# Rotary products of the queries on four column groups of TensorE, and weight preparation that waits for its own loads

## The chip, the core and the metric

The kernel runs on one core of a Trainium2 chip. A core has five engines that run side by side, each with its own stream of instructions: PE (TensorE, matrix products), ACT (ScalarE, activation functions and copies), DVE (VectorE, elementwise work, scans, reductions), POOL (GpSimd, slower elementwise work) and SP (SyncE, which here only issues DMAs). They are tied together by semaphores alone. Products land in PSUM, which has eight banks of 128 partitions by 512 float32; everything else lies in SBUF, on 128 partitions. The metric is the device time of one execution in microseconds (us), lower is better.

## What is computed

Eight sequences of 512 tokens with 256 channels go through four blocks, each `x = x + layernorm(block(layernorm(x)))`:

```python
# 1 attention with a compressed key/value and one rotary part shared by all 16 heads
c_kv   = x @ W_kv_down                                   # 256 -> 128
k_rope = rotary(c_kv @ W_k_rope); q_rope = rotary(x @ W_q_rope)      # 32 wide
rotary(x) = concat([x1*cos - x2*sin, x2*cos + x1*sin])   # x1, x2 the halves of 32 channels
scores = (q . k per head + q_rope . k_rope) / sqrt(48);  causal softmax;  @ v;  @ W_o
# 2 feed-forward 256 -> 1024 -> 256, ternary weights rebuilt in the kernel
#   scale = mean|w| by row, tern = clip(round(w/scale)); h = x @ (tern*scale).T + gate * x @ v.T @ fast_b.T @ u.T
#   out = ternary(w_proj) @ relu(h)**2
# 3 mixer: z = conv(x @ W_in), decays by a running sum, cos and sin of k*theta, weighted prefix scans, silu, @ W_out
# 4 feed-forward relu(x @ W1 + b1) @ W2 + b2
```

## The kernel before

Three chains of work are woven into each engine's stream. Chain `a` is the attention of one sequence ("batch" b), chain `d` holds the dense parts of the other three blocks, chain `m` is the mixer. A fourth chain `p` prepares the weights once, at the start. While chain `a` works on batch b, chains `d` and `m` work on batches b-1 and b-2. `chains()` lists the items of each chain in order, and the table `MERGE` says for each engine how many items to take from which chain in turn ("a8 p a2" is eight items of `a`, one of `p`, two of `a`). An engine executes its stream strictly in this order: an item that must wait holds everything behind it on its engine. `merged()` expands the table and `run()` calls `do` for each item (or `prepare` for those of `p`), and `between()` once before the first item of `d` or `m`.

The attention of a batch begins with a prologue on PE: `xT` (transposes of the input), `ckv`, `q` (two halves), `qr` (the rotary query product), `k`, `kr` (the rotary key product), `v`, `base`. Its 32 rotary channels are needed twice, once plain and once with the halves swapped, so the weights `wqr` and `wkr` hold both versions, 64 columns. `rotate` on DVE then multiplies 32 partitions of the result with the cosines and the next 32 with the sines (both in the table `rope`), and adds the two (L1340, L1341, L1344). `base` (L910) multiplies the rotated queries by the rotated keys for each of the four blocks of 128 queries, up to the diagonal. A product takes one of three PSUM banks in turn and waits until the bank was emptied.

Then 40 units of scores follow: `S` (PE L922), a fused add and maximum on DVE (L1410), the exponential on ACT (L1176), `T` (transposes, PE L930, copied by ACT L1183), `PV` (PE L948), which writes four groups of 32 columns of the array in turn. Queries and keys for `S` are split in three bf16 pieces by ACT (L1162, L1165), DVE (L1356) and POOL (L755, L757), sent to DRAM (L685) and read back into the tile `stack` (L636, six DMAs for a group of four heads).

The mixer of a batch takes on ACT the waves `fold`, `cos`, `sin` (L1239, L1243, L1246), on DVE `turn`/`frac` (L1468, L1478), `scan` (L1487) and `mix` (L1496) in 16 units of two scans and one mix, and on PE four `gather` (L1016). The ring of wave tiles is small: the `turn` of channels 4 to 7 needs gathers 0 and 1 first. In batches 0 and 7 `turn` is done by ACT (L1234). ACT holds one table set at a time; changing between exponential and sine is an instruction of its own, ACT_TABLE_LOAD.

At the start SP issues 33 loads in one row. Those for the attention count on the semaphore `loaded_first`. All others, from the ternary weights `raw_fc` to the bias `b2r`, count on one semaphore `loaded`, and the preparation on PE (L1049), ACT (L1272), POOL (L802) and DVE (L1533) waits until all of them have landed. Preparation works as `ternary` (ACT sums |w|, L1274; POOL compares and scales, L809 to L818), `prep` 0 to 15 (PE products and transposes, copied out by ACT or DVE) and `tables`.

## Time and profile before

| | us |
|---|---|
| median of 3 runs | 1410.93 |
| lowest and highest run | 1410.14, 1413.29 |
| the profiled execution | 1407.21 |
| its span, from first to last instruction | 1405.4 |

The profile is of one execution, so sums of durations are held against 1407.21; 1.8 us of it lie outside the span. It is 3.7 us below the median of the runs. The profile lists busy time by engine and by source line, a timeline, what each engine waited for, and the chain of work that ended last. PE is busy 87% of the span, DVE 78%, ACT 75%, POOL 24%, and the mean granted TensorE clock is 0.949 of the full one. Chains `d` and `m` have no work in the first 100 us; chain `a` has none after about 1180 us, when the mixers of batches 6 and 7 and their dense parts still run.

### The profile page before, as it was taken

To read this page: it belongs to the slowest core of one execution; us is meant where nothing else is said; L and a number is where in the kernel's file an instruction comes from. 1 tells how busy PE (TensorE), PEld (TensorE's weight loads), DVE (VectorE), ACT (ScalarE), POOL (GpSimd) and SP (SyncE) were. 2 spreads that over 40 slices of the span, in tenths; PEclk is the share of its full clock that TensorE was granted. 3 is DMA by queue.
4 is the path that set the end of the run, shared out by engine and by line. 5 is a ranking of instruction groups with operands and counts; after the bars stand their busy time and mean duration, and the time that the engine had idled before them with its cause. 6 is when DMAs were issued, how large, how long until landed. Compare 5 with 4: busy or idle time off the path is not lost.

```text
span 1405.4 us, 22661 instructions
## 1 busy us (share of the span) xinstructions
PE 1227.4 (87%) x7820; PEld 774.3 (55%) x7820; DVE 1101.7 (78%) x2259; ACT 1054.7 (75%) x2107; POOL 336.7 (24%) x317
## 2 busy tenths in 40 slices
PE   5889987888899998999999997998999998874767
PEld 2565664364546565666646764565646755542444
DVE  3683358779988988988888997898788998998940
ACT  4784789689789878798778888597778889547532
POOL 3943203400121303220134001430032201511021
PEclk9799999999999999999999999999999999996879
DMA  8404114412252105520334131511352131103000
GB/s 260 99 13 101 28 24 137 108 50 61 70 135 61 31 1 150 130 53 1 124 80 107 24 100 45 136 31 24 108 124 57 31 92 47 45 19 126 23 16 15
DMA packets 72019, 101.49 MB, mean 72 GB/s; under 512 B 10641, under 2 KB 44065, under 8 KB 71905
## 3 DMA queue, kind: packets, MB, share of 16 engines
q1 hardware_dynamic: 71904, 100.03, 27.2%
q8 instruction: 64, 1.05, 0.3%
q14 instruction: 51, 0.41, 0.1%
HBM read 74.31 MB, written 25.69 MB: 71 GB/s over the span
## 4 chain that ended last, share of the span: by engine, by line
PE 46%; DVE 21%; ACT 19%; issue 9%; DMA 2%; SPq 2%; POOL 1%; DVEq 0%; POOLq 0%; ACTq 0%
PE ps L865 15%; PE ps L875 12%; DVE work L1487 8%; PE ps L930 5%; ACT work L1176 5%; ACT work L1183 3%; PE ps L922 3%; PE ps L948 3%; DVE work L1410 3%; PE ps L1016 3%; DVE work L1496 2%; DVE work L1478 2%; ACT xnd L1119 2%; DVE work L1468 1%; PE ps L857 1%
## 5 line engine op out<-in xcount | busy, mean ns | idle before, releaser
L1487 DVE TENSOR_TENSOR_SCAN work<-work 128x512 f32<-128x512 f32 x256 | 313.2, 1254 | 23.0 <-ACT work L1243 21.0
L1410 DVE CUSTOM_DVE_ANT_0 work<-ps,work 128x384 f32<-128x384 f32 (+3 forms) x512 | 228.9, 486 | 109.9 <-PE ps L922 106.5
L1176 ACT ACTIVATE work<-work 128x384 f32<-128x384 f32 (+3 forms) x512 | 264.4, 560 | 44.9 <-DVE work L1410 44.1
L746 POOL TENSOR_TENSOR later_norms<-later_norms,singles 128x2 f32<-128x2 f32 x112 | 97.0, 867 | 711.6 <-ACT xnd L1119 428.5
L930 PE MATMUL ps<-ident,work 128*128 128x128 f32 x1280 | 202.4, 284 | 23.7 <-ACT work L1183 11.0
L930 PEld LDWEIGHTS ps<-ident,work 128*128 128x128 f32 x1280 | 152.6, 145 | 82.5 <-issue 33.5
L1183 ACT COPY work<-ps 128x512 f32<-128x512 f32 x300 | 170.9, 576 | 8.6 <-PE ps L930 8.3
L1496 DVE TENSOR_TENSOR work<-work 128x1024 f32<-128x1024 f32 x128 | 160.7, 1255 | 4.0
L922 PE MATMUL ps<-work 96*128 96x384 bf16 (+3 forms) x512 | 124.8, 311 | 29.9 <-ACT work L1183 28.0
L865 PE MATMUL ps<-led_xTd,wfc 128*128 128x512 f32 x256 | 122.3, 615 | 0.8 <-ACT led_xTd L1103 0.8
L875 PE MATMUL ps<-wf,hid 128*128 128x256 f32 x512 | 114.1, 383 | 5.5 <-issue 5.5
L875 PE MATMUL ps<-wpr,hid 128*128 128x256 f32 x512 | 114.7, 383 | 4.1 <-POOL hid L766 4.1
L865 PE MATMUL ps<-led_xTd,wf 128*128 128x512 f32 x256 | 115.8, 609 | 1.4 <-issue 1.4
L875 PEld LDWEIGHTS ps<-wf,hid 128*128 128x128 f32 x512 | 97.6, 192 | 21.2 <-issue 8.0
L875 PEld LDWEIGHTS ps<-wpr,hid 128*128 128x128 f32 x512 | 97.1, 192 | 19.2 <-POOL hid L766 5.9
L766 POOL TENSOR_TENSOR hid<-hid 128x512 f32<-128x512 f32 x64 | 79.9, 1258 | 111.7 <-ACT hid L1198 111.5
L1478 DVE SCALAR_TENSOR_TENSOR work<-work,smalls 128x512 f32<-128x512 f32 x128 | 97.3, 804 | 6.0 <-ACT work L1234 3.6
L948 PE MATMUL ps<-work 128*32 128x128 f32 x2560 | 93.4, 284 | 0.4 <-ACT work L1183 0.4
L922 PEld LDWEIGHTS ps<-work 96*128 96x128 bf16 x512 | 43.1, 99 | 84.2 <-ACT work L1183 40.4
L1239 ACT ACTIVATE work<-work 128x1024 f32<-128x1024 f32 x64 | 67.2, 1058 | 26.1 <-DVE work L1478 25.9
L865 PEld LDWEIGHTS ps<-led_xTd,wf 128*128 128x128 f32 x256 | 49.2, 195 | 64.4 <-issue 63.7
L1016 PE MATMUL ps<-work,sel 128*32 128x512 f32 x512 | 63.1, 610 | 19.1 <-DVE work L1496 18.9
(174 smaller groups left out, 1967.4 us busy)
## 6 DMA issues: line engine op xcount, KB each, us to landing
work<-values SPq DMA_DIRECT2D x64, 256.0 KB, 3.3
work<-ratios SPq DMA_DIRECT2D x64, 256.0 KB, 3.3
scratch<-work SPq DMA_DIRECT2D x32, 384.0 KB, 4.5
work<-scratch SPq DMA_DIRECT2D x64, 192.0 KB, 3.9
work<-scratch SPq DMA_DIRECT2D x64, 128.0 KB, 4.2
x_in<-x SPq DMA_DIRECT2D x8, 512.0 KB, 7.0
work<-scratch SPq DMA_DIRECT2D x64, 64.0 KB, 4.3
values<-work SPq DMA_DIRECT2D x16, 256.0 KB, 2.8
```

What stands on the lines that cost most here:

```text
L865: i = mm(dst, l, r, start=j == 0, stop=j == len(pairs) - 1)
L875: i = mm(ps[:, bank(b, name), t * D:(t + 1) * D], lhs[:, j, tt * P:(tt + 1) * P], rhs[:, j, :], start=j == 0, stop=j == n_k - 1)
L922: i = mm(out_of(b, name)[:, at:at + nk], stack[0:SROWS, hg % 2, 0, j, qt * P:(qt + 1) * P], stack[0:SROWS, hg % 2, 1, j, 0:nk], start=True ...
L930: i = tr(ps[:, bank(b, name), t * P:(t + 1) * P], sc[:, n % 4, t * P:(t + 1) * P], ident[:])
L948: i = mm(ps[32 * j:32 * j + 32, PV, qt * P:(qt + 1) * P], v_all[:, v0:v0 + 32], pt[:, (hg * UNITS + u) % 6, at + t * P:at + (t + 1) * P], ...
L1016: i = mm(ps[l * W:(l + 1) * W, bank(b, f"mem{quad}"), :], sel[:], ring[:, at, m, :], start=half == 0 and m == 0, stop=half == 1 and m == M ...
L1176: i = s_.activation(part_of, part_of, ACT.Exp, scale=-1.0, bias=nmax[:, row:row + 1])
L1183: s_.copy(pt[:, n % 6, 0:nk], out_of(b, name)[:, 0:nk]).then_inc(*drains(b, name))
L1410: i = v_.tensor_tensor_reduce(sc[:, n % 4, at:at + nk], out_of(b, name)[:, at:at + nk], base_of(qt), -SCORE_SCALE, BIG, ALU.add, ALU.min, ...
L1478: i = v_.scalar_tensor_tensor(ring[:, SIN_HALF[r], m, :], kvr[:, slot, :], turns[:, r, m:m + 1], whole[:, COS_HALF[r], m, :], ALU.mult, AL ...
L1487: v_.tensor_tensor_scan(ring[:, at, m, :], pwr[:, slot, :], ring[:, at, m, :], 0.0, ALU.mult, ALU.add).then_inc(*scanned.one)
L1496: v_.tensor_tensor(both, both, qc[:, half * MH:(half + 1) * MH], ALU.mult).then_inc(*mixed.one)
```

## The change

1. **qr**: instead of two products of 64 columns by 512 tokens, eight of 32 columns by 256 tokens. Column groups 0 and 1 hold the plain product for tokens 0 to 255 and 256 to 511, groups 2 and 3 the swapped one. The three DVE instructions of the rotation then work on 64 partitions by 256 instead of 32 by 512.
2. **kr**: the same four groups, but each over all 512 tokens (the second row of groups holds them with the halves of the tokens exchanged), eight products of 32 by 256 instead of one of 64 by 512. DVE's three instructions stay 512 long, on 64 partitions.
3. **base**: queries of the second half of the tokens lie on partitions 32 to 63; their blocks take two products instead of one (six in all instead of four, over the same columns).
4. **Loads**: a new semaphore `loaded_raw` counts the five loads of the ternary preparation. PE, ACT, POOL and DVE wait for it where they waited for `loaded`; `tables` and `between` wait for `loaded`. The table `rope` grows from 64 to 128 partitions.
5. **MERGE** is new for all five engines: the same items in the same order within each chain, woven differently.

The diff, with the tables of item 5 left out but for a line (the places where they matter are shown below it):

```diff
 MERGE = {
     "pe":
-        "a8 p a2 p a4 p4 a34 p a24 p a37 p a p3 a p a p a p a7 p a6 d5 a3 d a3 d a4 d a4 d a5 d a13 d a3 d a3 "
+        "a5 p a3 p a6 p4 a34 p a24 p a31 p3 a6 p a p a p a p a p a5 d a2 d a2 d a4 d6 a3 d a6 d a3 d a6 d a12 "
...
-        rope = sb("rope", [2 * DR, T])
+        rope = sb("rope", [4 * DR, T])
...
-            load(raw_fc, w_fc.rearrange("(g p) i -> p g i", p=P))
...
+            raw(raw_fc, w_fc.rearrange("(g p) i -> p g i", p=P))
+            raw(raw_pr, w_proj.rearrange("(g p) i -> p g i", p=P))
+            raw(raw_u, u.rearrange("(g p) r -> p g r", p=P))
+            raw(raw_fb[0:RANK], fast_b)
+            raw(raw_v[0:RANK], v)
...
-                        pool.wait_ge(loaded, 16 * n_rest[0])
+                        pool.wait_ge(loaded_raw, 16 * n_raw[0])
+                        pool.wait_ge(loaded_ident, 16)
...
                 if item == "qr":
-                    product(b, "qr", out_of(b, "qr")[0:2 * DR],
-                            [(wqr[:, c].rearrange("p s r -> p (s r)"), xa_c[c]) for c in range(DC)])
+                    may_fill(pe, b, "qr")
+                    for c in range(DC):
+                        for g in range(4):
+                            h = g % 2
+                            i = mm(out_of(b, "qr")[g * DR:(g + 1) * DR, 0:T // 2], wqr[:, c, g // 2, :],
+                                   xa_c[c][:, h * T // 2:(h + 1) * T // 2], start=c == 0, stop=c == DC - 1)
+                    i.then_inc(*fills(b, "qr"))
...
                 if item == "kr":
-                    product(b, "kr", out_of(b, "kr")[0:2 * DR], [(wkr[:].rearrange("p s r -> p (s r)"), ckv)])
+                    may_fill(pe, b, "kr")
+                    for h in range(2):
+                        for g in range(4):
+                            of = (h + g) % 2
+                            i = mm(out_of(b, "kr")[g * DR:(g + 1) * DR, h * T // 2:(h + 1) * T // 2], wkr[:, g // 2, :],
+                                   ckv[:, of * T // 2:(of + 1) * T // 2], start=True, stop=True)
+                    i.then_inc(*fills(b, "kr"))
...
                 if item == "base":
...
-                    product(b, f"base{n}", out_of(b, f"base{n}")[:, 0:(n + 1) * P],
-                            [(qrope[0:DR, n * P:(n + 1) * P], krope[0:DR, 0:(n + 1) * P])])
+                    name, h = f"base{n}", n // 2
+                    may_fill(pe, b, name)
+                    queries = qrope[h * DR:(h + 1) * DR, n % 2 * P:(n % 2 + 1) * P]
+                    if h == 1:
+                        mm(out_of(b, name)[:, 0:T // 2], queries, krope[DR:2 * DR, T // 2:T], start=True, stop=True)
+                    first, n_key = h * T // 2, (n % 2 + 1) * P
+                    i = mm(out_of(b, name)[:, first:first + n_key], queries, krope[h * DR:(h + 1) * DR, 0:n_key],
+                           start=True, stop=True)
+                    i.then_inc(*fills(b, name))
...
                 if n == 0:
-                    pe.wait_ge(loaded, 16 * n_rest[0])
+                    pe.wait_ge(loaded_raw, 16 * n_raw[0])
...
             def between():
+                pe.wait_ge(loaded, 16 * n_rest[0])
...
-            def rotate(b, name, dst):
+            def rotate(b, name, dst, n):
                 is_filled(dve, b, name)
-                v_.tensor_tensor(rtmp[0:DR, 0, :], out_of(b, name)[0:DR], rope[0:DR, :], ALU.mult)
...
+                v_.tensor_tensor(rtmp[0:2 * DR, 0, 0:n], out_of(b, name)[0:2 * DR, 0:n], rope[0:2 * DR, 0:n], ALU.mult)
+                v_.tensor_tensor(rtmp[0:2 * DR, 1, 0:n], out_of(b, name)[2 * DR:4 * DR, 0:n], rope[2 * DR:4 * DR, 0:n], ALU.mult
```

**ACT, at the start of the program, before.** L1162 are the two casts of the queries, L1165 those of the keys, L1274 the sums of |w|, L1279 and L1281 an exponential and a logarithm for the tables, L1169 the copies of `v`, L1286 and L1288 copies for `prep`, L1176 the first exponentials of the scores.

```order
L1098 COPY xTa<-ps 128x512 x2
L1162 CAST work<-ps 128x512 x2
L1165 CAST work<-ps 128x512 x2
L1274 ACTIVATE wpr,work<-work 128x256 x8
L1169 COPY work<-ps 128x32x16 x2
L1279 ACTIVATE work<-work 128x1
L1281 ACT_TABLE_LOAD
L1281 ACTIVATE work<-work 128x1
L1274 ACTIVATE wpr,work<-work 128x1024 x2
L1286 COPY work<-ps 16x512 x2
```

The same place after (the same items are now at L1125, L1189, L1192, L1301, L1306, L1308, L1313):

```order
L1125 COPY xTa<-ps 128x512 x2
L1301 ACTIVATE wpr,work<-work 128x256 x8
L1189 CAST work<-ps 128x512 x2
L1306 ACTIVATE work<-work 128x1
L1308 ACT_TABLE_LOAD
L1308 ACTIVATE work<-work 128x1
L1192 CAST work<-ps 128x512 x2
L1301 ACTIVATE wpr,work<-work 128x1024 x2
L1313 COPY work<-ps 16x512 x2
L1196 COPY work<-ps 128x32x16 x2
```

The eight sums of |w| stand ahead of the casts of the queries, and the exponential and the logarithm ahead of those of the keys.

**PE, in the mixer and dense work of the last batch, before.** L1016 is a `gather`, L875 with `wout` the output product of the mixer of batch 6, L857 transposes, L865 and L875 with `wf` the last feed-forward of batch 6 (`gc`, `gproj`).

```order
L875 MATMUL ps<-wout,work 128x256 x8
L1016 MATMUL ps<-work,sel 32x512 x8
L857 MATMUL ps<-ident,xnd 128x128 x8
L865 MATMUL ps<-led_xTd,wf 128x512 x6
L1016 MATMUL ps<-work,sel 32x512 x8
L865 MATMUL ps<-led_xTd,wf 128x512 x10
L875 MATMUL ps<-wf,hid 128x256 x16
L1016 MATMUL ps<-work,sel 32x512 x8
L875 MATMUL ps<-wf,hid 128x256 x16
L1016 MATMUL ps<-work,sel 32x512 x8
L875 MATMUL ps<-wout,work 128x256 x8
```

The same place after (L1016 is now L1042, L857 and L865 are L865 and L873, L875 is L883):

```order
L883 MATMUL ps<-wout,work 128x256 x8
L865 MATMUL ps<-ident,xnd 128x128 x8
L873 MATMUL ps<-led_xTd,wf 128x512 x16
L1042 MATMUL ps<-work,sel 32x512 x8
L883 MATMUL ps<-wf,hid 128x256 x32
L1042 MATMUL ps<-work,sel 32x512 x24
L883 MATMUL ps<-wout,work 128x256 x8
```

The first gather of batch 7 has moved behind all eight `gc` products of batch 6, and the other three behind its `gproj`.

**ACT, the same stretch, before.** L1234 are `turn`s, L1239, L1243 and L1246 the waves of batch 7, L1119 with `ps` and with `x` the statistics of batch 6.

```order
L1234 ACTIVATE work<-work,smalls 128x512 x8
L1239 ACTIVATE work<-work 128x1024 x2
L1223 COPY work<-ps 128x512 x2
L1243 ACT_TABLE_LOAD
L1243 ACTIVATE work<-work,singles 128x1024 x2
L1246 ACTIVATE work<-work 128x1024 x2
L1239 ACTIVATE work<-work 128x1024 x2
L1243 ACTIVATE work<-work,singles 128x1024 x2
L1246 ACTIVATE work<-work 128x1024 x2
L1119 ACTIVATE xnd,later_norms<-ps,singles 128x256 x4
```

The same place after (turns L1261, waves L1266, L1270, L1273, statistics L1146):

```order
L1261 ACTIVATE work<-work,smalls 128x512 x2
L1146 ACTIVATE xnd,later_norms<-ps,singles 128x256 x4
L1261 ACTIVATE work<-work,smalls 128x512 x2
L1146 ACTIVATE xnd,later_norms<-x,singles 128x256 x4
L1137 ACTIVATE xnd<-x,later_norms 128x256 x2
L1266 ACTIVATE work<-work 128x1024 x2
L1130 COPY led_xTd<-ps 128x2x256
L1137 ACTIVATE xnd<-x,later_norms 128x256 x2
L1270 ACT_TABLE_LOAD
L1270 ACTIVATE work<-work,singles 128x1024
```

The statistics and the norms of batch 6 have moved ahead of the first waves of batch 7. Over the whole program ACT's stream held 37 table loads before and holds 33 after.

## Rows read from the trace of the kernel before

**Rows 1.** The page: the span, and the busy time of the engines.

```profile
span 1405.4 us, 22661 instructions
PE 1227.4 (87%) x7820; PEld 774.3 (55%) x7820; DVE 1101.7 (78%) x2259; ACT 1054.7 (75%) x2107; POOL 336.7 (24%) x317
```

**Rows 2.** Stretches: us; busy of PE, PEld, DVE, ACT, POOL (instructions); clock, DMA share, GB/s.

```profile
0.00:100.00 100.00, 77.48 (x639) 50.53 (x640) 63.96 (x222) 63.64 (x138) 64.47 (x57) 0.88 0.49 131
100.00:200.00 100.00, 92.30 (x604) 61.56 (x603) 38.45 (x131) 66.87 (x152) 21.05 (x24) 0.97 0.25 54
200.00:300.00 100.00, 83.93 (x479) 48.88 (x478) 82.88 (x163) 81.41 (x149) 30.96 (x28) 0.95 0.39 104
300.00:400.00 100.00, 84.50 (x681) 53.87 (x680) 85.75 (x197) 85.10 (x177) 12.72 (x16) 0.95 0.21 59
400.00:500.00 100.00, 93.42 (x577) 60.49 (x576) 89.08 (x166) 80.97 (x150) 21.52 (x19) 0.98 0.29 67
...
1200.00:1300.00 100.00, 69.32 (x277) 40.75 (x276) 91.06 (x101) 61.47 (x109) 25.96 (x20) 0.86 0.20 64
```

**Rows 3.** The chain that ended last, in its first 60 us: start, us, what.

```profile
20.00 8.75 DMA b2r<-b
...
45.73 0.55 PE ps L922
```

**Rows 4.** DMAs: issue on SP's timeline; KB each and us to landing.

```profile
13.24 1.45 SPq L621 DMA_DIRECT2D work<-v  x1
...
work<-v SPq DMA_DIRECT2D x1, 16.0 KB, 5.2
...
38.33 0.89 SPq L636 DMA_DIRECT2D work<-scratch  x2
...
work<-scratch SPq DMA_DIRECT2D x2, 64.0 KB, 5.0
```

**Rows 5.** Timeline of the start: start, us, engine, line; idle before and what ended it.

```profile
20.37 0.59 ACT L1162 CAST work<-ps 128x512 bf16<-128x512 f32 x1 [6.03 <-PE ps L865]
...
28.77 0.42 ACT L1274 ACTIVATE wpr<-work 128x256 f32<-128x256 f32 x1 [2.32 <-DMA b2r<-b]
...
29.42 1.41 POOL L757 TENSOR_TENSOR work<-xna,work 128x512 bf16<-128x512 f32 x1
```

**Rows 6.** Groups by line and shape, count, busy us, mean ns of one, idle before.

```profile
L1243 ACT ACT_TABLE_LOAD x17 | 21.8, 1283 | 0.3
...
L948 PE MATMUL ps<-work 128*32 128x128 f32 x2560 | 93.4, 284 | 0.4 <-ACT work L1183 0.4
...
L1016 PE MATMUL ps<-work,sel 128*32 128x512 f32 x512 | 63.1, 610 | 19.1 <-DVE work L1496 18.9
...
L865 PE MATMUL ps<-xTa,wqr 128*64 128x512 f32 x32 | 15.4, 605 | 0.0
...
L1424 DVE TENSOR_TENSOR xna<-ps,work 128x256 f32<-128x256 f32 x32 | 13.6, 425 | 1.1
L1341 DVE TENSOR_TENSOR work<-ps,rope 32x512 f32<-32x512 f32 x16 | 10.9, 682 | 0.2
...
L865 PE MATMUL ps<-work,wkr 128*64 128x512 f32 x16 | 8.6, 618 | 1.9 <-DVE work L1341 1.9
```

**Rows 7.** PE's timeline in the second attention: transposes, then PV, then scores.

```profile
152.29 0.60 PE L930 MATMUL ps<-ident,work 128*128 128x128 f32 x4
152.82 1.09 PE L948 MATMUL ps<-work 128*32 128x128 f32 x32
```

**Rows 8.** Timeline of DVE and of PE in the mixer of batch 7.

```profile
1256.00 1.22 DVE L1496 TENSOR_TENSOR work<-work 128x1024 f32<-128x1024 f32 x1
...
1275.90 2.34 DVE L1487 TENSOR_TENSOR_SCAN work<-work 128x512 f32<-128x512 f32 x2 [2.17 <-ACT work L1243]
...
1344.26 1.23 DVE L1496 TENSOR_TENSOR work<-work 128x1024 f32<-128x1024 f32 x1
...
1292.45 3.38 PE L1016 MATMUL ps<-work,sel 128*32 128x512 f32 x16 [13.33 <-DVE work L1496]
```

More of the change, by code:

```diff
@@ L508, in sandwich_kernel @@
         loaded_wo = sem("loaded_wo")
+        loaded_raw = sem("loaded_raw")
         loaded = sem("loaded")
@@ L625, in first, with raw @@
                 load(dst, src, loaded_first, n_first)
+            def raw(dst, src):
+                load(dst, src, loaded_raw, n_raw)
             def load_x(b):
@@ L1336, in summed @@
                 dve.sem_inc(*drains(b, name))
-            def rotate(b, name, dst):
+            def rotate(b, name, dst, n):
                 is_filled(dve, b, name)
-                v_.tensor_tensor(rtmp[0:DR, 0, :], out_of(b, name)[0:DR], rope[0:DR, :], ALU.mult)
-                v_.tensor_tensor(rtmp[0:DR, 1, :], out_of(b, name)[DR:2 * DR], rope[DR:2 * DR, :], ALU.mult
+                v_.tensor_tensor(rtmp[0:2 * DR, 0, 0:n], out_of(b, name)[0:2 * DR, 0:n], rope[0:2 * DR, 0:n], ALU.mult)
+                v_.tensor_tensor(rtmp[0:2 * DR, 1, 0:n], out_of(b, name)[2 * DR:4 * DR, 0:n], rope[2 * DR:4 * DR, 0:n], ALU.mult
                                  ).then_inc(*drains(b, name))
                 is_drained(dve, b, name)
-                v_.tensor_tensor(dst[0:DR], rtmp[0:DR, 0, :], rtmp[0:DR, 1, :], ALU.add).then_inc(*rope_ready.one)
+                v_.tensor_tensor(dst[0:2 * DR, 0:n], rtmp[0:2 * DR, 0, 0:n], rtmp[0:2 * DR, 1, 0:n], ALU.add
+                                 ).then_inc(*rope_ready.one)
                 need_given(dve, rope_ready)
@@ L1389, in do @@
                         dve.wait_ge(loaded_first, 16 * n_first[0])
-                    rotate(b, "qr", qrope)
+                    rotate(b, "qr", qrope, T // 2)
                 if item == "k":
@@ L1393, in do @@
                 if item == "kr":
-                    rotate(b, "kr", krope)
+                    rotate(b, "kr", krope, T)
                 if item == "base":
@@ L1588, in tables @@
     cos, sin = np.cos(freqs).T, np.sin(freqs).T
-    rope = np.concatenate([cos, cos, -sin, sin]).astype(f32)
+    plain, swapped = np.concatenate([cos, cos]), np.concatenate([-sin, sin])
+    rope = np.concatenate([plain, np.roll(plain, T // 2, 1), swapped, np.roll(swapped, T // 2, 1)]).astype(f32)
     p = np.arange(P)
```

12 lines of the change are left out of this document (5 added, 7 removed), and 86 rows, old and new, of the table MERGE.

## The prediction, made before the changed kernel ran

> **What bounds the kernel now.** I read the page first. PE is busy 1227 of 1405 us, DVE 1102, ACT 1055 [rows 1]: no engine is idle enough to be forgotten, and PE comes first. Then the stretches of 100 us [rows 2]. They show four stages. From 0 to 100 only the attention of batch 0 and the preparation run, and PE is busy 77%. From 100 to 200 PE is at 92% and DVE at 38%: the mixer has not begun. From 200 to 400 PE falls to 84% while DVE and ACT are at 81 to 86%: the first mixers have come in and each engine waits for another. From 400 on PE is at 93%. After 1200 DVE is at 91% and PE at 69%: the mixers of batches 6 and 7 bound the end. So in the middle an edit is worth what it takes from PE, at the end what it takes from DVE's chain of scans. The first stretch has a bound of its own: the chain that ended last begins with the loads, whose last (`b2r`, issued at 20.00) lands at 28.75, and runs through the preparation to the first scores at 45.73 [rows 3].
>
> **The start.** The last of the five loads of the preparation is issued at 13.24 and lands 5.2 us later, at 18.4 [rows 4]. So PE, ACT and POOL may prepare 10.3 us earlier than at 28.75. Not all of that is gained, since two other things are late next. The first is queued work. ACT now does the eight sums of |w| ahead of the query casts: the sums come every 0.40 us, 3.2 us in all, from 18.4 to about 21.7, and the first cast began at 20.37 [rows 5]; it slips by 1.3 us, and POOL and the DMAs behind it. POOL ended the last key piece at 30.8 (29.42 + 1.41) [rows 5], after a DVE that did 2.05 us of rotation first; with 0.8 us less rotation and POOL's gaps closed I get 30.2 to 30.5, so 0.3 to 0.6 us earlier. The second is the stack. The last two of the first six DMAs into it are issued from 38.33 on (the second at 38.8) and land 5.0 us later, at 43.8 [rows 4]; they hang on the key pieces. The scores began at 45.7, so at most 1.9 us came from the preparation. The first scores then start at about 43.4: **2 us** earlier. Bounds: 0 (the later query cast delays everything) and 5 (what PE did not do in the first attention because of the preparation's products among it, whose place moves little).
>
> **The rotary products.** `qr` has 4 records per batch, 15.4 us in 8 batches, 1.93 each; `kr` 8.6, so 1.07 each [rows 6]: 3.00 us together. After, both are eight products of 32 columns over 256 tokens. The trace has the same form twice. The gather, four column groups over 512, costs 63.1 us for 256 products, 0.246 each, so 0.123 for 256 columns; PV, over 128, costs 93.4 us for 1280, 0.073, so 0.146 for 256 [rows 6]. Sixteen of them cost 1.97 to 2.34 us. That is 0.66 to 1.03 us less per batch, nearly all on `qr`; `base` passes the same columns with six products instead of four, for which I add 0.1. On DVE, the three instructions of the query rotation fall from 0.68 us (512 long) to 0.43, the nearest row of 256 [rows 6]: 0.8 us per batch, and in the prologue PE waits for that chain (`kr` for the bank that `rotate` empties, 1.9 us in all [rows 6]). Seven batches outside the start: PE 7 x 0.75 = 5.2 us, of which at 93% busy most shows; DVE another 5.6, mostly hidden behind PE. I take **4 us**. Bounds: 11 (both in full) and -3.
>
> The lower bound is from what the change of form costs. A T group whose next is another T or S starts it 0.44 us later; before PV it is 0.53 (152.29 to 152.82 [rows 7]), so 0.09 us for going to narrow groups. Two products of this kind per batch, entered and left, are 4 x 0.09 x 8 = 3 us if nothing of it was paid before.
> The Trainium skill, TensorEngine Tiling (Array Packing), Key Properties, says that changing the tiling mode drains the engine; it speaks against this change. By it the 4 us would be about 1; by the row, where leaving PV shows no gap and `wqr` was 64 wide and switched already, they stay near 4.
>
> **Table loads.** ACT has 37 before and 33 after, 1.283 us each [rows 6]: 5.1 us of ACT. ACT is not the bound in the middle but the exponential and copy of the scores feed PE; **1 us** shows. Bounds 0 and 5.
> The Trainium skill, ScalarE: Activation LUTs, What ACT_TABLE_LOAD costs, puts a switch at about 2.66 us with its drain, which would make it 10.6 us of ACT; the trace has no such second part (idle before 17 loads is 0.3 us in all [rows 6]), so the 5.1 stays.
>
> **Where the mixer starts.** The order puts the dense part of batch 0 four items of `a` earlier on PE, its second convolution 38 items earlier on DVE (194 to 156), the first scan nine earlier, and the last scan of batch 0 29 earlier (287 to 258). DVE's idle time at 100 to 200 (61.5 us) is thus used, and the crowd at 200 to 400 thinned. From batch 2 on the orders keep step within ten items. If 200 to 400 came to the 93.4% of 400 to 500, PE's 168.4 us would take 180: 20 us gained at most; the least is 0, since the scans cannot start before their waves, and ACT's waves now stand between exponentials. I take **5 us**, a quarter, because DVE and ACT are at 83 to 86% there and stay so.
>
> **The end.** Here the order works against the change. The mixer of batch 7 begins with its first scan at 1275.90, 18.7 us after the last mix of batch 6 (1256.00 + 1.22), and ends with the mix at 1344.26 [rows 8]; DVE is its bound, at 3.51 us for a unit of two scans and a mix. After, ACT does the statistics and norms of batch 6 ahead of the first cosine: eight Square reductions of 0.6 us, two norms, two folds, and the wait for the sums on DVE and the power on POOL between them. Adding them up from the same last mix, the first cosine is ready 27 us after it, not 18.7: 8 us lost. Of that some comes back: two sums (about 2.2 us) no longer lie between the scans, the first gather (1292.45, after 13.33 us of idle PE [rows 8]) stands later but DVE reaches `frac` 4 later still, which ends a stall of 1.4, and the exponential set's load before `tanh` is out of the way. **Lost: 4 us.** Bounds 0 and 8 (a PE at half clock makes the `wout` product 6.6 us rather than 3.6 and holds the statistics 2 us more).
>
> **The sum.** -2 - 4 - 1 - 5 + 4 = -8 us: the profiled 1407.2 would be 1399, and the median 1410.9 becomes **1403**. The rest of the new weave moves hundreds of items by a few places; its own waits (PE idles some 7% at 400 to 500) can fall either way by about 7 us, which I count in the range alone.
>
> **The rivals.**
> Slower by the end and the weave (18%): the last mixer starts its full 8 us late and PE, idle longer, falls to half clock there (it is 0.86 at 1200 to 1300 [rows 2]), while the mixer at 200 to 400 gives nothing. Then -2 - 4 - 1 + 0 + 8 and 7 from the weave: 1419. It decides once the loss at the end exceeds the 7 us of start, rotary and table loads. For it: the orders of the last stretch. Against: most of DVE's chain there is unchanged.
> Taken back (18%): start and rotary are real but waited away elsewhere, since the chain of waits turns from engine to engine; 1408 to 1414.
> The fill gives more (16%): 200 to 400 comes near the steady share, 12 us or more instead of 5: 1388 to 1394.
> The column groups do not overlap (3%): the sixteen products would then cost what a single one of their length does, half of a 512-long product's 0.86 (two records, 0.43 apart), 6.9 us per batch instead of 2.1; 7 x 4.8 = 34 us, about 1437. PV and gather [rows 6] say that they do overlap.
> My forecast, 1394 to 1408, holds 44%, and 1% is left for slips.
>
> **How the numbers follow.** Faster by over 0.2% (below 1408.1, about what a measurement of this kernel can tell from no change): 44 + 16 = 60%. Within 0.2%: 18%. Slower: 22%. The range reaches to 1389 and 1417: it leaves out the best of the fill case, the worst of the slow one, and the case of no overlap.
>
> **What would show it.** In the profile after: the first score product at 43 to 44 us, with the waits of PE and ACT on `b2r` gone; `qr` and `kr` each near 1.0 to 1.2 us per batch; the three instructions of the query rotation near 0.43 us; 33 table loads of 1.28; PE above 84% at 200 to 400; the time from the last mix of batch 6 to the first scan of batch 7 at 25 to 28 us instead of 18.7. The forecast is wrong if the end of the last attention does not come 10 us or so earlier, or if the stretch behind it grows by much more than 4 us.

## The result, and the profile after

Over 20 runs each, the changed kernel took 1407.17 us in the median (1401.80 to 1409.79) and the kernel before 1411.53 (1402.47 to 1414.65). The ratio is **0.9974, 95% interval 0.9963 to 0.9986**: faster, by 3.7 us with an interval of 2 to 5. The forecast was 1403. It had the direction right, but its sum gave a gain of 8 us, more than twice the measured one. The profiled execution took 1407.72 us, its span is 1405.9; the profiled one of before was 4 us under its own median, so the two profiles show the same length and the gain has to be looked for in stretches.

The page after, answering to [rows 1]. PE is busy 10.8 us less, DVE 12.6:

```profile
span 1405.9 us, 23146 instructions
PE 1216.6 (87%) x8060; PEld 778.2 (55%) x8060; DVE 1089.1 (77%) x2259; ACT 1052.2 (75%) x2103; POOL 333.9 (24%) x317
```

The stretches after, with the columns of [rows 2]:

```profile
0.00:100.00 100.00, 75.35 (x675) 50.06 (x676) 62.58 (x222) 63.56 (x140) 64.56 (x57) 0.90 0.50 132
100.00:200.00 100.00, 95.21 (x649) 63.67 (x647) 47.65 (x148) 69.02 (x156) 23.16 (x28) 1.00 0.36 86
200.00:300.00 100.00, 73.47 (x457) 46.20 (x456) 79.09 (x152) 85.46 (x147) 27.54 (x25) 0.86 0.26 64
300.00:400.00 100.00, 90.06 (x733) 57.27 (x735) 81.68 (x195) 86.80 (x185) 9.63 (x11) 0.97 0.24 65
...
1200.00:1300.00 100.00, 80.85 (x298) 44.72 (x297) 83.24 (x90) 61.23 (x108) 21.95 (x18) 0.88 0.18 56
```

PE at 200 to 400 has *not* risen: 163.5 us against 168.4. At 1200 to 1300 DVE has gone from 91 to 83: it waits where it was the bound.

Groups by line and shape, answering to [rows 6] (L907 is now `qr`, L919 `kr`, L1368 and L1369 the two products of the rotation):

```profile
L1270 ACT ACT_TABLE_LOAD x15 | 19.2, 1283 | 0.3
L1203 ACT ACT_TABLE_LOAD x14 | 18.0, 1283 | 0.3
...
L907 PE MATMUL ps<-xTa,wqr 128*32 128x256 f32 x128 | 8.6, 385 | 0.0
L919 PE MATMUL ps<-work,wkr 128*32 128x256 f32 x128 | 8.6, 385 | 0.0
...
L1369 DVE TENSOR_TENSOR work<-ps,rope 64x256 f32<-64x256 f32 x8 | 3.4, 426 | 0.1
```

`qr` costs 1.07 us per batch instead of 1.93. The mixer of batch 7 on DVE, answering to [rows 8]. Columns are start, us, engine, line, idle before and what ended it; L1516 is a scan, L1525 a mix, L1547 a sum of batch 6 (`gystats`), L1530 the `gate`, L1534 the product with the silu:

```profile
1247.27 1.22 DVE L1525 TENSOR_TENSOR work<-work 128x1024 f32<-128x1024 f32 x1
...
1275.27 2.34 DVE L1516 TENSOR_TENSOR_SCAN work<-work 128x512 f32<-128x512 f32 x2 [5.96 <-ACT work L1270]
...
1301.45 0.68 DVE L1547 TENSOR_TENSOR xnd<-ps,b2r 128x512 f32<-128x512 f32 x1
...
1307.83 0.69 DVE L1547 TENSOR_TENSOR xnd<-ps,b2r 128x512 f32<-128x512 f32 x1
...
1313.14 0.69 DVE L1530 TENSOR_TENSOR work<-ps,work 128x512 f32<-128x512 f32 x1 [3.10 <-PE ps L1042]
...
1344.09 1.22 DVE L1525 TENSOR_TENSOR work<-work 128x1024 f32<-128x1024 f32 x1
...
1348.92 0.69 DVE L1530 TENSOR_TENSOR work<-ps,work 128x512 f32<-128x512 f32 x1 [3.61 <-PE ps L1042]
...
1350.74 1.23 DVE L1534 SCALAR_TENSOR_TENSOR work<-work 128x1024 f32<-128x1024 f32 x1 [1.12 <-ACT work L1277]
```

The last mix of batch 6 ends at 1248.49, 8.7 us earlier than in [rows 8]. The first scan of batch 7 comes at 1275.27, nearly where it was: **26.8 us behind the mix instead of 18.7**. A lead of 8.7 us is gone in one gap. Earlier, the attention of batch 7 had ended even sooner: its transposes `attnT` are at 1151.46 on PE, before at 1169.04.

### The profile page after: what moved, and what is told of

Read it like the earlier page. It is cut to its first block, busy times and chain, and to the rows that moved or that the text cites. A ratio compares the mean times of both kernels' runs of the same rounds, so it can differ in the third digit from the quotient of the medians.

```text
span 1405.9 us, 23146 instructions
## 1 busy us (share of the span) xinstructions
PE 1216.6 (87%) x8060; PEld 778.2 (55%) x8060; DVE 1089.1 (77%) x2259; ACT 1052.2 (75%) x2103; POOL 333.9 (24%) x317
## 4 chain that ended last, share of the span: by engine, by line
PE 54%; DVE 16%; ACT 16%; issue 6%; POOL 5%; SPq 1%; DMA 1%; POOLq 0%; DVEq 0%; ACTq 0%
PE ps L873 19%; PE ps L883 15%; PE ps L956 5%; DVE work L1516 4%; ACT work L1203 4%; PE ps L1042 4%; DVE work L1439 3%; PE ps L974 3%; PE ps L948 3%; ACT work L1210 3%; DVE work L1507 2%; ACT xnd L1146 2%; DVE work L1525 2%; PE ps L865 1%; DVE work L1394 1%
## 5 line engine op out<-in xcount | busy, mean ns | idle before, releaser
L1516 DVE TENSOR_TENSOR_SCAN work<-work 128x512 f32<-128x512 f32 x256 | 313.1, 1255 | 39.5 <-ACT work L1270 37.8
L1525 DVE TENSOR_TENSOR work<-work 128x1024 f32<-128x1024 f32 x128 | 160.0, 1250 | 4.3
L873 PE MATMUL ps<-led_xTd,wf 128*128 128x512 f32 x256 | 120.3, 621 | 3.9 <-issue 3.9
L873 PE MATMUL ps<-led_xTd,wfc 128*128 128x512 f32 x256 | 118.0, 596 | 0.0
L883 PE MATMUL ps<-wpr,hid 128*128 128x256 f32 x512 | 115.4, 385 | 2.5 <-POOL hid L772 2.5
L883 PE MATMUL ps<-wf,hid 128*128 128x256 f32 x512 | 114.8, 385 | 0.8 <-issue 0.8
L883 PEld LDWEIGHTS ps<-wf,hid 128*128 128x128 f32 x512 | 98.7, 194 | 15.9 <-issue 2.5
L883 PEld LDWEIGHTS ps<-wpr,hid 128*128 128x128 f32 x512 | 97.4, 193 | 17.2 <-POOL hid L772 3.6
L1266 ACT ACTIVATE work<-work 128x1024 f32<-128x1024 f32 x64 | 67.1, 1055 | 40.3 <-DVE work L1507 40.1
L1042 PE MATMUL ps<-work,sel 128*32 128x512 f32 x512 | 67.2, 646 | 31.7 <-DVE work L1525 31.6
L873 PEld LDWEIGHTS ps<-led_xTd,wf 128*128 128x128 f32 x256 | 49.4, 199 | 62.2 <-issue 62.1
```

The lines of the kernel that those rows point to most:

```text
L873: i = mm(dst, l, r, start=j == 0, stop=j == len(pairs) - 1)
L883: i = mm(ps[:, bank(b, name), t * D:(t + 1) * D], lhs[:, j, tt * P:(tt + 1) * P], rhs[:, j, :], start=j == 0, stop=j == n_k - 1)
L1042: i = mm(ps[l * W:(l + 1) * W, bank(b, f"mem{quad}"), :], sel[:], ring[:, at, m, :], start=half == 0 and m == 0, stop=half == 1 and m == M ...
L1516: v_.tensor_tensor_scan(ring[:, at, m, :], pwr[:, slot, :], ring[:, at, m, :], 0.0, ALU.mult, ALU.add).then_inc(*scanned.one)
L1525: v_.tensor_tensor(both, both, qc[:, half * MH:(half + 1) * MH], ALU.mult).then_inc(*mixed.one)
```

## The experiments

The two orders can be cut and joined. At four places of the attention's chain both have done the same items on every engine: in the scores of batch 0, at the end of those of batch 3, at the end of those of batch 5, and, but for five items, behind the last attention (what follows is the *tail*). So the order can be undone stretch by stretch. "O" is a stretch in the old order, "N" in the new one. Ratios are to the kernel before, with 95% intervals:

| kernel | code | start | b0-3 | b4-5 | b6-7 | tail | ratio | interval |
|---|---|---|---|---|---|---|---|---|
| before | old | O | O | O | O | O | 1 | |
| rotary_only | rotary | O | O | O | O | O | 0.9978 | 0.9955 to 1.0002 |
| loads_only | loads | O | O | O | O | O | 0.9987 | 0.9967 to 1.0007 |
| order_new_only | old | N | N | N | N | N | 1.0082 | 1.0052 to 1.0112 |
| code_old_order | new | O | O | O | O | O | 0.9934 | 0.9905 to 0.9962 |
| new_b0_to_b3 | new | O | N | O | O | O | 0.9891 | 0.9871 to 0.9912 |
| old_start_new_to_b5 | new | O | N | N | O | O | 0.9888 | 0.9863 to 0.9912 |
| old_start_old_tail | new | O | N | N | N | O | 0.9896 | 0.9866 to 0.9926 |
| after_old_start | new | O | N | N | N | N | 0.9956 | 0.9937 to 0.9975 |
| **after** | new | N | N | N | N | N | 0.9974 | 0.9963 to 0.9986 |
| tail_before | new | N | N | N | N | O | 0.9913 | 0.9881 to 0.9945 |
| new_to_b5_old_after | new | N | N | N | O | O | 0.9893 | 0.9869 to 0.9917 |
| old_order_new_tail | new | O | O | O | O | N | 1.0038 | 1.0021 to 1.0056 |
| waves_first | new | N | N | N | N | mixed | 1.0081 | 1.0058 to 1.0104 |

**Code and order apart.** The first kernel has the whole code and the old tables, the second the new tables and the old code:

```diff
 MERGE = {
     "pe":
-        "a5 p a3 p a6 p4 a34 p a24 p a31 p3 a6 p a p a p a p a p a5 d a2 d a2 d a4 d6 a3 d a6 d a3 d a6 d a12 "
+        "a8 p a2 p a4 p4 a34 p a24 p a37 p a p3 a p a p a p a7 p a6 d5 a3 d a3 d a4 d a4 d a5 d a13 d a3 d a3 "
...
```

> The whole code of the change (rotary products on four column groups, loads on their own semaphore) in the old order of all five engines. The theory of the forecast: the rotary gives 4 us and the start up to 2, both come from the code and do not need the new order, so 1405.5 us against 1411.5 before, a ratio of 0.9957. In the trace PE's first score product comes before 45.7 us, since nothing stands ahead of the casts of the queries, and qr takes 1.07 us per batch. The rival: the saved time of PE is waited away again in the old order, which was written for the old durations; then 1410 to 1412, a ratio of 0.999 to 1.000, and the 4.3 us of the change come from the order.

> The new order of all five engines with the old rotary products and the old wait of the preparation for all loads. By the forecast the order is worth -1 (table loads) -5 (more work at 200 to 400) +4 (the end) = -2 us: 1409.5, a ratio of 0.9985. If the order brings the whole gain it is 1407, 0.997. If it brings nothing, or costs, 1411.5 or more: a ratio of 1.000 to 1.003. In this kernel ACT has the eight sums of |w| ahead of the casts of the queries and these wait for b2r (28.8 us): the first score product then comes at 50 us or later instead of 45.7, a loss of 5 us or so which the change itself does not have, so the ratio as measured holds that loss too: 1.002 by the forecast.

The code in the old order gave 9.3 us, more than both theories. The first score product came at 43.02, as expected. The new order alone cost 11.6: its first scores came at 53.91 instead of 45.66, so, if all of that delay shows at the end, some 8 of these are the start that waits for `b2r`; about 3 are then left as the order's own loss, where the forecast had a gain of 2.

**The two edits of the code, each alone.**

```diff
-            load(raw_fc, w_fc.rearrange("(g p) i -> p g i", p=P))
+            raw(raw_fc, w_fc.rearrange("(g p) i -> p g i", p=P))
...
-                        act.wait_ge(loaded, 16 * n_rest[0])
+                        act.wait_ge(loaded_raw, 16 * n_raw[0])
```

> The kernel before with nothing but the new rotary products (qr, kr, base and rotate) in the old order, with the old waits. By the forecast -4 us: 1407.5, a ratio of 0.9972. PE's busy time falls by 6 to 7 us, DVE's by 5 or 6. If the saving is taken back by other waits: 1410.5 to 1411.5, 0.9993 to 1.0. What the same code gives beyond this with the loads split, in the old order, is the worth of the start.

> The kernel before with nothing but the five loads of the ternary preparation on their own semaphore: old rotary products, old order. By the forecast's term for the start 2 us less, a ratio of 0.9986, with the first score product at 43.5 us. The difference of the two kernels measured in the old order (0.9934 with both edits, 0.9978 with the rotary alone) would make it 0.9956, 6 us. A third possibility: SP's issue of fast_b varies (2.69 to 4.95 us in the profiles), the landing of b2r with it (28.75 and 30.8 us), and the profile of before had an early one; then the wait that is removed is worth 3 to 5 us on average, 0.9965 to 0.998.

3.1 and 1.8 us, each with an interval of 3 us to either side: near the forecast's 4 and 2, and neither told from zero by itself. Their sum is 4.9, both together gave 9.3; the intervals overlap, and whether the rest is chance stays open. PE's busy time fell by 4.2 us in the profile of rotary_only, less than the 6 to 7 expected, although `qr` and `kr` alone gave 6.8 (24.0 to 17.2). `base`, now with a product more on two blocks, did not take it back: its records, counted without their overlaps, cover 22.0 us of PE before, 20.7 in rotary_only and 18.6 in after. (The groups by shape can't be added up here, since products of different shapes run side by side.) In after two of them, on partitions 0 to 31 and 32 to 63, start 0.01 us apart:

```profile
126.78 0.37 PE L938 MATMUL ps<-work 32*128 32x128 f32 x1
126.79 0.48 PE L936 MATMUL ps<-work 32*128 32x256 f32 x1
```

The clock can account for what is missing: over the whole span PE was busy for 117 us at the lower of its two levels in rotary_only, for 107 before. By the 16 `wout` products of the kernel before, which took 3.62 us at 1159 with a granted clock of 1.00 and 6.56 at 1272 with 0.56, ten such us more are some 5 us of busy time (an estimate).

**The tail.** In PE's table, from after to tail_before (the other engines likewise):

```diff
-d10 m d5 m d16 m d2 m3 d13
+d10 m d5 m d6 m d5 m d6 m d m d13
```

> The kernel after, but behind the last attention item each engine runs the remaining items in the order of the kernel before. What changes: on ACT the statistics and norms of batch 6 go back behind the first waves of the mixer of batch 7, on PE the gathers of batch 7 go back ahead of the gc and gproj products of batch 6. Theory 1 (the forecast's): these statistics hold up the first cosine by 8 us, so the time from the last mix of batch 6 to the first scan of batch 7 falls from 26.8 us to 19, and all of it shows, since the mixer of batch 7 bounds the end: 1399 to 1401 against 1407.2, a ratio to before of 0.992. Theory 2: the first scan of batch 7 came at 1275.9 before and at 1275.3 after, and something that both share holds it there (the dense part of batch 7 or PE's work behind the last attention); then it stays at 1275 or a little under, and the time at 1405 to 1407, 0.996 to 0.997.

> The code of the change in the old order, with only the items behind the last attention in the new order: the reverse of tail_before. If the new order of the tail costs the same whatever stands before it: 8 to 9 us more than 1400.1 (the kernel without it), a ratio to before near 0.9995, with 27 us from the last mix of batch 6 to the first scan of batch 7. By the forecast, in which half of the 8 us come back: 1404, 0.9963. If the cost in the changed kernel came from the earlier end of its attention, and not from this order: 1400 to 1401, 0.994.

In tail_before theory 1 held, in time and in the gap. In old_order_new_tail its gap held (27 us), but the time is 1.0038 where it had 0.9995. DVE in tail_before: the last mix of batch 6, then the first scan of batch 7, 17.6 us behind its end:

```profile
1244.30 1.23 DVE L1524 TENSOR_TENSOR work<-work 128x1024 f32<-128x1024 f32 x1
...
1263.16 2.34 DVE L1515 TENSOR_TENSOR_SCAN work<-work 128x512 f32<-128x512 f32 x2 [2.07 <-ACT work L1269]
```

And in old_order_new_tail, 26.9 us behind it:

```profile
1249.66 1.23 DVE L1522 TENSOR_TENSOR work<-work 128x1024 f32<-128x1024 f32 x1
...
1277.76 2.34 DVE L1513 TENSOR_TENSOR_SCAN work<-work 128x512 f32<-128x512 f32 x2 [5.96 <-ACT work L1267]
```

The old tail gives 0.0061 of the time, 8.6 us; by after_old_start against old_start_old_tail it is 0.0060. Put behind the old order the new tail costs 0.0104, with 9.4 us between the profiles' spans (1399.2 and 1408.6). So the price belongs to the tail's order, whatever stands before it. Its size is less sure: 0.0104 is 14.7 us, and each of these differences has an uncertainty of some 5 us.

**Statistics or gathers?** The new tail has the statistics of batch 6 ahead of the waves of batch 7 on ACT, and the gathers of batch 7 behind the `gc` products on PE. waves_first undoes only the first (and on DVE puts the two sums of batch 6 back behind scan 6). ACT's table (`m14` are turn 3 and the folds, cosines, sines 0 to 3 with what followed them; `d16` statistics, norms and `gc`):

```diff
-m d2 m d3 m2 d2 m d m4 d m d m d m d m d m d3 m4
+m14 d16 m4
```

> The kernel after, with one move in the tail: on ACT the folds, cosines and sines 0 to 3 of batch 7 stand ahead of the statistics of batch 6 again, and on DVE the two sums of batch 6 behind scan 6 of batch 7. PE is left as it is, so the gathers of batch 7 still stand behind all gc products of batch 6. Theory 1: the statistics ahead of the first cosine are the whole cost of the tail, and the gap from the last mix of batch 6 to the first scan of batch 7 falls to 18 or 19 us: 1397 to 1399, as tail_before. Theory 2: the place of the gathers costs by itself: gc of batch 6 comes later behind the waves, gather 0 and 1 behind gc, turn 4 behind them, and DVE waits there for 3 to 8 us: 1401 to 1406.

Neither number held: it is *slower* than after, 11 us by the profiles' spans (1416.7 against 1405.9) and 15 by the ratios, by theory 2's mechanism and far beyond its size. The first scan did come 21 us behind the last mix (1245.27 to 1266.13). Then DVE stands still (L1506 is the `frac` of turn 4, L1041 on PE a gather, L872 `gc`):

```profile
1305.97 1.42 DVE L1506 SCALAR_TENSOR_TENSOR work<-work,smalls 128x512 f32<-128x512 f32 x2 [19.83 <-ACT work L1260]
```

```profile
1286.25 16.38 PE L872 MATMUL ps<-led_xTd,wf 128*128 128x512 f32 x32 [0.72 <-issue]
1302.56 1.92 PE L1041 MATMUL ps<-work,sel 128*32 128x512 f32 x16
```

The gather waits behind all eight `gc`, 16.4 us of them, these behind the norms, and turn 4 behind the gather. So in the new tail the early statistics are what keeps the late gathers harmless: the statistics cannot be put back alone. Both undone, the tail is 8.6 us shorter. No run put only the gathers back, so how the 8.6 us divide between the two stays open.

**The fill of batches 0 to 3, and the rest of the weave.** The tables are made of pieces. In shorthand, with `n` an item's number in the attention's chain (486 is the end of batch 3, 738 that of batch 5):

```diff
-MERGE = old                                      # code_old_order
+MERGE = old[:60] + new[60:486] + old[486:]       # new_b0_to_b3
+MERGE = new[:738] + old[738:]                    # new_to_b5_old_after
+MERGE = old[:60] + new[60:738] + old[738:]       # old_start_new_to_b5
```

> The code of the change in the old order, with the new order only from the first scores of batch 0 to the end of batch 3 (at both ends the two orders have done the same items). This is the stretch of which the forecast took 5 us: the fill. By the forecast 1400.1 - 5 = 1395, a ratio of 0.990. By the traces, in which the rotary product of batch 4 came 7.8 us earlier while the start lost 1.4, it is worth 9: 1391, 0.9865. If PE's share of 73% at 200 to 300 means that the fill gives nothing: 1400, 0.9934.

> The kernel after, with the old order on all engines from the end of the scores of batch 5 on, where both orders have done exactly the same items (behind S39 of batch 5); the new order stands before it. Theory 1, from the traces: at the keys' rotary product of batch 6 the new order is 12.3 us ahead of the old one (872.5 against 884.8), and from there to the last mix of batch 6 the old order takes 366.2 us and the new one 373.0, so the lead is not lost any more: about 7 us under the kernel with only its tail in the old order (1396.6), 1388 to 1391, a ratio to before of 0.986. Theory 2: the lead is one of the PE stream alone, and DVE's mixers are behind by as much; then the end takes it all back and this is 1396 to 1400, like the two kernels measured.

> As new_to_b5_old_after, and also the first 60 items of attention in the old order on all engines: the casts of the queries and keys stand ahead of the sums of |w| on ACT again. Theory 1: the first score product comes at 43 us instead of 44.3 to 45.2, and the end of the first attention at 100 instead of 101.4 to 102.8, so 1.5 to 2.5 us less than new_to_b5_old_after, 1387 to 1389. Theory 2: the start is waited away later: the same as new_to_b5_old_after.

new_b0_to_b3 is 0.0043 under code_old_order, 6.1 us where the forecast had 5. It and the other two are the fastest kernels of the study, 1393 us each, 1.1% under the kernel before and 0.8% under the changed one. Batches 4 and 5 in the new order add nothing (0.9891 and 0.9888). new_to_b5_old_after, at 1393.5, met neither of its theories (1388 to 1391, 1396 to 1400), and old_start_new_to_b5 came out the same, as its theory 2 had it. From where do the 6 us come? Not from idle time. From PE's first scores to the `kr` of batch 4 both kernels do the same 3444 PE instructions, in 525.5 and 518.4 us. PE is busy 467.5 and 461.2 us of it, so its idle time is the same 58 and 57: the *busy* time shrank. The groups of PE in that stretch that shrank most are `fc` and `fproj`. In code_old_order:

```profile
L870 PE MATMUL ps<-led_xTd,wfc 128*128 128x512 f32 x96 | 48.9, 652 | 0.8 <-ACT led_xTd L1127 0.8
L880 PE MATMUL ps<-wpr,hid 128*128 128x256 f32 x192 | 45.4, 397 | 1.9 <-POOL hid L769 1.9
```

In new_b0_to_b3:

```profile
L871 PE MATMUL ps<-led_xTd,wfc 128*128 128x512 f32 x96 | 43.9, 596 | 0.0
L881 PE MATMUL ps<-wpr,hid 128*128 128x256 f32 x192 | 42.6, 380 | 0.4 <-POOL hid L770 0.4
```

The same products, 7.8 us cheaper (others became somewhat dearer). The `fc` of batch 0 shows one reason, first in code_old_order, then in new_b0_to_b3:

```profile
130.64 8.47 PE L870 MATMUL ps<-led_xTd,wfc 128*128 128x512 f32 x12 [0.77 <-ACT led_xTd L1127]
```

```profile
124.54 1.88 PE L871 MATMUL ps<-led_xTd,wfc 128*128 128x512 f32 x4
128.35 10.57 PE L871 MATMUL ps<-led_xTd,wfc 128*128 128x512 f32 x24
```

0.71 us for a record in the one, 0.44 to 0.47 in the other. The granted clock at 100 to 160 is 0.91 in the first kernel and 1.00 in the second:

```profile
100.00:160.00 60.00, 56.62 (x311) 34.76 (x313) 21.29 (x66) 36.68 (x80) 18.42 (x20) 0.91 0.33 76
```

```profile
100.00:160.00 60.00, 58.99 (x276) 40.17 (x277) 18.12 (x51) 33.28 (x78) 19.42 (x22) 1.00 0.28 62
```

In finer stretches of code_old_order, PE was busy 3.19 of 5 us at 125 to 130, waiting for ACT, and the `fc` then ran at half clock until about 137:

```profile
125.00:130.00 5.00, 3.19 (x15) 1.95 (x13) 1.50 (x5) 2.61 (x8) 0.71 (x1) 0.66 0.93 236
130.00:135.00 5.00, 4.36 (x5) 1.85 (x6) 0.00 (x0) 1.06 (x2) 0.00 (x0) 0.50 1.02 218
```

The new order does not have less of the low clock; it has it where PE has little to do. In new_b0_to_b3:

```profile
200.00:250.00 50.00, 28.59 (x251) 20.69 (x252) 42.80 (x83) 45.30 (x80) 5.74 (x6) 0.73 0.13 43
```

From the first scores to the `kr` of batch 4 the clock was at its lower level for 49.5 us in code_old_order, with PE busy in 43.5 of them, and for 52.8 us in new_b0_to_b3, with PE busy in 36.6. At half speed the 6.9 us less are worth some 3.5 of the 6.4 us of busy time (an estimate). Where the rest comes from stays open, and this account is read from one profile of each kernel, not shown by a run of its own.

**The start, and batches 6 and 7.** On ACT:

```diff
-a3 p a2 p a2 p4 a2 p6 a80
+a7 p a2 p11 a80
```

> The kernel after, with the first 60 items of attention in the old order on all engines: on ACT the casts of the queries and keys stand ahead of the eight sums of |w| again. Theory 1, from the profiles so far: the first score product came at 43.25 on average in five kernels with the split loads and the old start, and at 45.7 in five with the new start, and all of the 2.5 us show at the end: 1404.5, a ratio to before of 0.9955, against 0.9974 for the kernel after. Theory 2: they are waited away behind it, as the medians of new_to_b5_old_after and old_start_new_to_b5 (both 1393.5) would have it: 0.9974 again.

> As after_old_start, and the items behind the last attention in the old order too, so the new order stands from the first scores of batch 0 to the end of the last attention. It differs from old_start_new_to_b5 (0.9888) in batches 6 and 7 alone. Theory 1: the new order of that stretch costs what the traces show (373.0 us from the rotary product of batch 6 to the last mix of batch 6 instead of 366.2, of which some came back): 3 us more, 0.991. Theory 2: it costs nothing that shows: 0.9885 to 0.9890.

after_old_start came out as theory 1 had it, 0.9956, and the two other pairs that differ in the start give 0.0017 and 0.0005: on average 0.0013, 1.9 us, though each difference alone is within its interval. The profile says how. ACT in the kernel after, the first sum of |w| and the casts of the queries:

```profile
20.07 0.42 ACT L1301 ACTIVATE wpr<-work 128x256 f32<-128x256 f32 x1 [5.47 <-DMA work<-v]
...
23.28 1.04 ACT L1189 CAST work<-ps 128x512 bf16<-128x512 f32 x2
```

and in code_old_order:

```profile
21.41 0.59 ACT L1186 CAST work<-ps 128x512 bf16<-128x512 f32 x1 [6.89 <-PE ps L870]
```

POOL ends the key pieces at 32.33 in after and at 30.57 there, 30.83 before. The scores of batch 0 begin on PE when their DMA has landed, in after:

```profile
45.16 1.89 PE L948 MATMUL ps<-work 96*128 96x512 bf16 x4 [4.45 <-DMA work<-scratch]
```

0.6 us earlier than in [rows 3]. old_start_old_tail against old_start_new_to_b5 is 0.9896 against 0.9888: batches 6 and 7 in the new order cost nothing that these runs can tell. The interval of the first, 0.9866 to 0.9926, leaves room for both theories.

**Do the column groups work side by side?**

```diff
-                    for c in range(DC):
-                        for g in range(4):
+                    for g in range(4):
+                        for c in range(DC):
```

> The kernel after, with the eight products of qr in another order: the two that add up in one column group stand side by side (group 0 twice, then 1, 2, 3) instead of going round the four groups. If the low price (1.07 us for eight) comes from column groups working at the same time, then neighbours in one group cannot, and qr takes 1.5 to 2 us per batch, kr still 1.07. If eight products of 32 columns are cheap for another reason, it stays at 1.07. The time of the whole kernel: up to 5 us more.

```diff
                     may_fill(pe, b, "qr")
+                    for _ in range(8):
+                        mm(out_of(b, "qr")[0:DR, 0:T // 2], wqr[:, 0, 0, :], xa_c[0][:, 0:T // 2], start=True, stop=True)
```

> The kernel after, with eight more products in each qr, all of them the first product of column group 0 again (32 columns by 256 tokens; they are overwritten by the right ones). If the low price of eight products on four groups, 1.07 us or 0.134 each, comes from groups working side by side, eight in one group cost what a product of their length costs alone, half of 0.97 (two products of 512 by 64 columns took 1.93 us): 3.4 to 3.9 us more per batch. If a product of 32 columns is cheap by itself, they cost 1.0 to 1.1 us more.

The first left `qr` at 1.09 us, against what its first theory expected (ratio 0.9980, 0.9963 to 0.9997). The second cost 29.1 us in 8 batches, 3.64 each (L905 are the added products), as "side by side" would have it:

```profile
L905 PE MATMUL ps<-xTa,wqr 128*32 128x256 f32 x128 | 29.1, 380 | 0.0
L909 PE MATMUL ps<-xTa,wqr 128*32 128x256 f32 x128 | 11.6, 384 | 0.0
```

Both hold together, since PE starts a product of another group while one of the first is still waiting. In qr_group_by_group, at 120.3 us, the 16 records still start in four bursts of four, each burst within 0.04 us. PE's timeline in the kernel with eight more, the products of L909 beginning before the last of L905:

```profile
122.92 0.42 PE L909 MATMUL ps<-xTa,wqr 128*32 128x256 f32 x3
123.12 0.38 PE L905 MATMUL ps<-xTa,wqr 128*32 128x256 f32 x1
123.16 1.21 PE L909 MATMUL ps<-xTa,wqr 128*32 128x256 f32 x13
```

The whole kernel took 1430.0 us in its one run, 22.9 over the median of after: of 29 us put on PE, about 79% show.

## Why the prediction was wrong, and where it was right

By its own terms, in us of 1411; measured values are differences of two kernels of the table, with some 3 to 5 us of uncertainty each:

| term | forecast | measured |
|---|---|---|
| rotary and loads, in the old order | -6 | -9.3 (code_old_order) |
| start, what the new order takes back | in the -2 | +1.9 to 2.5 |
| table loads | -1 | not apart, in the order's terms |
| fill, batches 0 to 3 | -5 | -6.1 |
| weave of batches 4 to 7 | 0 (7 either way) | +0.7 (-0.4 and +1.1) |
| end | +4 | **+8.6** |
| sum | -8 | -3.7 |

The gain came out at less than half of the forecast because the terms missed in both directions. The end (4.6 us), the start (2 to 2.5), the table loads (up to 1) and the weave (0.7) cost more or gave less than forecast; rotary with loads (3.3) and fill (1.1) gave more. That 3.7 us of gain are left is in part this cancelling, and so luck.

- **The end is the step that failed**, and only in its size. The gap was forecast to grow by 8 us, to 25 to 28, and grew by 8.1, to 26.8. The mistake is the sentence "Of that some comes back". From the first scan to the product with the silu the mixer took 74.65 us before and 75.47 after, so nothing came back. (The 8.6 us of the table alone could not tell 8 from 4, with its uncertainty of some 5 us; these two times can.) The kernel before has, in that chain on DVE, the two sums `osum` (L1332), the two `gystats` (L1518), and the wait for the silu:

```profile
1287.67 0.85 DVE L1332 SCALAR_TENSOR_TENSOR x<-ps,later_norms,x 128x256 f32<-128x256 f32 x2
1288.73 0.88 DVE L1332 SCALAR_TENSOR_TENSOR x<-ps,later_norms,x 128x256 f32<-128x256 f32 x2 [0.21 <-DVE x L1332]
...
1345.40 0.68 DVE L1518 TENSOR_TENSOR xnd<-ps,b2r 128x512 f32<-128x512 f32 x1
1347.60 0.69 DVE L1501 TENSOR_TENSOR work<-ps,work 128x512 f32<-128x512 f32 x1 [1.52 <-PE ps L1016]
1350.55 1.22 DVE L1505 SCALAR_TENSOR_TENSOR work<-work 128x1024 f32<-128x1024 f32 x1 [2.26 <-ACT work L1250]
```

  The two `osum` did leave, 2.1 us with their waits, but the last `gystats`, which stood behind the last mix where DVE waits anyway, is now at 1307.83 between scans. The stall at `frac` 4 went from 1.41 to 1.14 us, not away. The exponential set's load did leave the place before `tanh` (that wait fell from 2.26 to 1.12), but the wait for the last gather ahead of it rose from 1.52 to 3.61 (0.7 of this only because the `gystats` no longer stands there), and that for gather 1 from 2.12 to 3.10. A wait of 0.95 us for a cosine is new, ahead of the fifth scan:

```profile
1283.42 2.34 DVE L1516 TENSOR_TENSOR_SCAN work<-work 128x512 f32<-128x512 f32 x2 [0.95 <-ACT work L1270]
```

  The forecast listed what left the chain and did not look at what moved in. Taking the full 8 would have given 1407, the measured time, but only because the other misses cancel.
- **Start.** "First scores at 43 to 44" was wrong for the changed kernel: 45.16, and 44.25 to 47.27 in five others with this start and the split loads. The slip of the casts was put at 1.3 us; measured against the same loads in the old order it is 1.9 (21.41 to 23.28) and against [rows 5] 2.9. SP's issue of `fast_b`, which took 2.69 us before, took 4.83 in this execution and held `v` back by 2.3 us. The step behind it failed: POOL's last key piece was forecast at 30.2 to 30.5 and ended at 32.33, and the DMA behind it with it. With the start in the old order the split loads did what was said: first scores at 41.7 to 44.5 in seven kernels against 45.66 and 48.18. The waits of PE and ACT on `b2r` are gone, as forecast.
- **Rotary.** `qr` and `kr` 1.07 us each (1.0 to 1.2 forecast), the two multiplications of the query rotation 0.41 and 0.43 us (0.43 forecast). The addition behind them is longer than the forecast had it on either side, 0.92 us before (not 0.68) and 0.59 after; the three together gave 0.85 us per batch, forecast 0.8. The whole edit gave 3.1 (forecast 4). `base` was put at 0.1 us more per batch and did not cost more: 22.0 us of PE before, 18.6 after, in all eight batches.
- **Fill.** The size held, the mechanism did not. PE "above 84% at 200 to 400" was the sign given; it is 81.8% in after, and the gain is there all the same. It comes in PE's busy time, not in its idle time, where the forecast had looked for it.
- **Table loads**: 33 of 1.283 us, as forecast.
- **The end of the last attention** comes 17.6 us earlier, 10 or so being demanded, and the stretch behind it grew by 18.0 (236.4 to 254.4), far more than 4: by this sign of its own the forecast is wrong. That this is still no loss of 14 us is seen in tail_before: 245.3 us behind an `attnT` at 1147.87. Nine of the 18 are only an attention that ran ahead of mixers which bound the end, and nine are the tail's order.
- **Rivals.** "Taken back" (1408 to 1414) came close in size, 1407.2 being measured, but it has start and rotary waited away, and in the old order these were there in full. "Slower by the end and the weave" named the mechanism that counted, the full 8 us at the end, and joined it with a fill of nothing and 7 us of weave, which did not come. "The column groups do not overlap" is refuted by 3.64 us for eight products in one group against 1.07 for eight on four.

## What to carry to other kernels

When a list of work is woven anew, cost at the end both what leaves the bounding chain and what moves into it; a saving inside a chain counts only if nothing else takes the place. Two orders that have done the same items at some point can be cut and joined there: eight such hybrids told gains from losses that the whole hid, and five of them are clear of both kernels. Judge a stretch by the time between two places at which the same work has been done, not by an engine's share of busy time.

## What the runs showed of the hardware

- PE starts matrix products on other column groups while one of the first group is pending: neighbours in one group cost nothing extra as long as others follow (1.09 against 1.07 us), eight more in that group alone cost 3.64. Products on different groups of 32 partitions start 0.01 us apart (`base`).
- `fc` products of one shape took 0.71 us a record where the granted clock was at its lower level for most of the time (0.50 at 130 to 135) and 0.44 to 0.47 at full clock. With about the same time at the lower level (49.5 and 52.8 us), PE was busy in 43.5 or 36.6 us of it, by the order of the work.
- The issue of one small DMA on SP (`fast_b`, 1 KB) took between 2.31 and 5.26 us in the profiles of this study (16 of them) and moved every load behind it: in the two with the old wait for all loads and the old start, 2.69 and 4.36 us, the first sum of |w| came at 28.77 and 30.86.
